# A two-layer vision block on one core: the end of a sample as a third line of steps beside the next sample's convolutions

## What is computed

```
h   = exp(d_t[..., None] * A) * h + (d_t * u_t)[..., None] * b_t[:, :, None, :]
y_t = einsum('bhkdn,bkn->bkd', h, c_t)        # over 4096 positions
yv  = ys[0] + flip(ys[2]) + wh2hw(ys[1]) + wh2hw(flip(ys[3]))
yv  = _ln(yv, out_norm_g, out_norm_b) * silu(z)
out = interleave(xl_out, yv @ out_proj_w.T) + x
```

## Time and profile before

| what | value |
|---|---|
| median of 3 runs (lowest to highest) | 19739.79 us (19717.09 to 19748.55) |
| profiled execution, its own time | 19722.72 us |
| its span, first to last instruction | 19720.9 us |
| busy share of the span: PE, DVE, ACT, POOL | 75%, 80%, 42%, 51% |
| DMA share of the 16 DMA engines | 61% |
| mean granted PE clock | 0.816 of 2.4 GHz |

### The profile page before, as it was taken

How to read it: one execution, slowest core, us unless ns; L and a number is a source line. 1 busy time by engine, 2 the same in 40 slices (tenths; PEclk the granted TensorE clock), 3 DMA queues, 4 the chain that set the end, 5 groups by cost and what they waited for, 6 DMA issues and landing times. The chain is left out here.

```text
span 19720.9 us, 211923 instructions
## 1 busy us (share of the span) xinstructions
PE 14827.0 (75%) x65784; PEld 6380.2 (32%) x65784; DVE 15739.8 (80%) x12143; ACT 8193.2 (42%) x14246; POOL 10055.0 (51%) x5172
## 2 busy tenths in 40 slices
PE   7877788587885879767796778958789487885655
PEld 4423432234322443234332333314333144321102
DVE  3338989789797897878877798878978779797995
ACT  3244335443354433634335443444334443354332
POOL 2125755457354563546644465444645447354663
PEclk9988898688986889868897788978889688886555
DMA  2226666666557665576655766556655666567775
GB/s 81 85 84 173 185 174 164 177 174 184 151 161 186 168 190 144 159 181 174 182 147 155 183 178 175 154 159 179 180 163 150 174 177 182 151 161 178 188 184 132
DMA packets 1510551, 3218.40 MB, mean 163 GB/s; under 512 B 238225, under 2 KB 669393, under 8 KB 1507921
## 3 DMA queue, kind: packets, MB, share of 16 engines
q1 hardware_dynamic: 1509456, 3204.84, 60.9%
HBM read 2473.07 MB, written 731.12 MB: 162 GB/s over the span
## 5 line engine op out<-in xcount | busy, mean ns | idle before, releaser
L1852 POOL TENSOR_TENSOR HC<-H,BR 128x1024 f32<-128x1024 f32 x3072 | 7317.8, 2384 | 5965.8 <-DVE H L1705 3282.9
L1705 DVE TENSOR_TENSOR_SCAN H<-dA,CR,PU 128x1024 f32<-128x1024 f32 x2304 | 5400.5, 2344 | 261.4 <-ACT CR L1080 58.8
L750 PE MATMUL PU<-PT,SELB 96*128 96x512 bf16 x6144 | 2264.8, 457 | 3143.6 <-DVE H L1705 2588.6
L1080 ACT ACTIVATE dA<-dA,A 128x1024 f32<-128x1024 f32 x3072 | 3506.1, 1143 | 2173.1 <-DMA dA<-dld 2149.3
L1449 DVE TENSOR_TENSOR PU<-PU,BR 128x1024 f32<-128x1024 f32 x3072 | 3731.9, 1215 | 420.4 <-PE PU L750 382.0
L750 PE MATMUL PB<-RA,RB 128*128 128x64 f32 (+4 forms) x11424 | 3881.5, 487 | 74.7 <-DVE RA L1452 43.5
L750 PE MATMUL PY<-HC,CB 128*32 128x256 f32 x24576 | 2397.1, 469 | 21.6 <-POOL HC L1852 18.8
L750 PEld LDWEIGHTS PB<-RA,RB 128*128 128x128 f32 (+3 forms) x11424 | 1753.8, 184 | 1899.6 <-issue 1766.7
L750 PEld LDWEIGHTS PU<-PT,SELB 96*128 96x128 bf16 x6144 | 501.3, 103 | 4720.3 <-issue 4128.5
L1705 DVE TENSOR_TENSOR_SCAN H<-dA,PU 128x1024 f32<-128x1024 f32 x768 | 1755.0, 2285 | 341.8 <-ACT CR L1080 228.5
L750 PE MATMUL PB<-RA 128*128 128x384 f32 (+2 forms) x4272 | 1760.9, 551 | 10.0 <-DVE T L1449 9.7
(11 more groups left out here) (165 smaller groups left out, 17187.5 us busy)
## 6 DMA issues: line engine op xcount, KB each, us to landing
dA<-dld SPq DMA_DIRECT2D x3072, 512.0 KB, 5.9
PT<-ptd SPq DMA_DIRECT2D x2304, 64.0 KB, 4.3
BR<-bcd SPq DMA_DIRECT2D x256, 512.0 KB, 7.3
ptd<-RA SPq DMA_DIRECT2D x176, 576.0 KB, 3.9
y0d<-RA SPq DMA_DIRECT2D x512, 192.0 KB, 8.0
RA<-y0d SPq DMA_DIRECT2D x128, 768.0 KB, 6.4
yd<-YS SPq DMA_DIRECT2D x768, 128.0 KB, 4.7
tkd<-RB SPq DMA_DIRECT2D x256, 262.0 KB, 4.8
```

Of the source, the lines that this page charges most:

```text
L750: return nc.tensor.matmul(out, w, x, start=start, stop=stop, skip_group_check=True)
L1080: return ac.activation(out, in_, f, **kw)
L1705: v.tensor_tensor_scan(h, a, x, 0.0 if first else K.CR[:, gi:gi + 1], MUL, ADD).then_inc(S["s_scan"], 1)
L1852: po.tensor_tensor(K.HC[:, w % NHC, :], K.H[:, w % NH, :], K.BR[:, (w // 24) % NBR, 1, :], MUL).then_inc(S["s_mulC"], 1)
```

## The change

**The lines.** The round has two lines now, `start` (a to f) and `end` (g and h). For the middle rounds a new set of tables, `AMID`, lays the steps of `end` between those of `start`, per engine. The result is laid between the scan's slots by new `TAKEN` tables. In the middle rounds the end stands where part d does. The end's own order changes too: the five stages `g.total`, `g.mean`, `g.var`, `h.gates` and `h.final` follow each other by strip, each one strip behind the one before.

**How many scans of a middle round stand in each part on DVE's list** (start, g and h are parts of their own before; after, g and h are in d's stretch):

| part | start | g | h | a | b | c | d | e | f |
|---|---|---|---|---|---|---|---|---|---|
| before | 8 | 20 | 18 | 55 | 141 | 32 | 56 | 53 | 5 |
| after | - | in d | in d | 51 | 140 | 57 | 68 | 49 | 19 |
| round 1, before | - | - | - | 67 | 141 | 62 | 63 | 45 | 8 |

**The end by strips.** The reciprocal root is taken strip by strip (two activations on 512 columns instead of two on 4096 for the whole). `XM` has three buffers of one strip; `SQ`, `RS`, `ZB`, `XB` and `LB` have one each. In a middle round the end's PSUM steps all use one bank (the third), and d's steps take turns on the other two. `g.begin` loads direction 3 whole (six DMAs of 512 KB), and direction 1 in eight pieces of three DMAs of 128 KB, five pieces at once and three after POOL has added the first three. POOL's eight adds are in groups of five and three.

**Smaller edits.** `d.in` loads straight into the padded image `YP` (rows of 64 elements, 256 bytes) and ACT works in place; before, it loaded strips of 512 elements into `XT`. The convolution weights of part d move from `RB` to `PX` and are padded from 96 to 128 output columns. `x1d` and `xld` get three buffers. `e.begin` waits for the end; `a.begin` no longer does.

```diff
     def last(self):
         yield from self.step("g.begin")
-        yield from self.woven(8, "g.load", "g.total", "g.mean", None, "g.var")
-        yield from self.step("g.rstd")
-        yield from self.woven(8, "h.load", "h.gates", "h.final")
+        stages = ("g.total", "g.mean", "g.var", "h.gates", "h.final")
+        for r in range(8 + len(stages)):
+            for q in range(len(stages) - 1, -1, -1):
+                if 0 <= r - q - 1 < 8:
+                    yield from self.step(stages[q], r - q - 1)
+            for name, i in (("g.load", r), ("h.load", r - 3), ("h.rest", r - 4)):
+                if 0 <= i < 8:
+                    yield from self.step(name, i)
...
+def merged(start, end, kind, engine):
+    left = iter(start)
+    steps = []
+    for step, n in zip(end, AMID.get((kind, engine), [0] * len(end))):
+        steps += itertools.islice(left, n)
+        steps.append(step)
+    out, left = [], iter(steps + list(left))
     slots = [("s", u, p) for u in range(NU + LAG + 1) for p in range(3)]
...
+                if pre and fin and step[0][0] in "gh":
+                    bank = NP - 1
+                else:
+                    turn = (turn + 1) % (NP - 1 if pre and fin and step[0][0] == "d" else NP)
+                    bank = turn
...
     def g_var(i, p):
         ac.wait_ge(*R.at("var", i + 1, "g"))
-        act(K.VR[:, strip(i)], R.bank(("g.var", i, 0))[0:96, :], ACT.Copy).then_inc(S["vr"], 1)
+        if i:
+            ac.wait_ge(S["h_n"], 2 * i)
+        else:
             ac.preload_act_table_set("natural_log_exp_and_others")
+        act(K.RS, R.bank(("g.var", i, 0))[0:96, :], ACT.Ln, bias=K.ONE[0:96, 1:2]).then_inc(S["vr"], 1)
+        ac.wait_ge(*R.at("vr", i + 1, "g"))
+        act(K.RS, K.RS, ACT.Exp, scale=-0.5).then_inc(S["rstd"], 1)
...
-            mm(o[:, 1::2], K.XT[:, i % 2, 0, s_], K.WP[:, 0:96], False, False)
+            mm(o[:, 1::2], K.XM[i % 3][:, s_], K.WP[:, 0:96], False, False)
...
-        dma(K.XT[:, i % 2, 0, :], K.x1d[par, 0, :, strip(i)], f"xt{i % 2}")
+        dma(K.YP[:, 0, 1 + 8 * i:9 + 8 * i, 1:65], rows8(K.x1d[b % 3, 0, :, strip(i)]), f"xin{i % 2}")
...
     def g_begin(_, p):
         if p:
             if p == 1:
-                po.wait_ge(S["gy"], 192)
+                po.wait_ge(S["gy"], 336)
+            if p == 6:
+                po.wait_ge(S["gy3"], 144)
             s = slice((p - 1) * 1024, p * 1024)
-            po.tensor_tensor(K.RB[0:96, s], K.RB[0:96, s], K.RA[0:96, s], ADD).then_inc(S["g_y13"], 1)
+            po.tensor_tensor(K.RB[0:96, s], K.RB[0:96, s], K.TY[(p - 1) % 5], ADD).then_inc(S["g_y13"], 1)
...
     def e_begin(_, p):
         if p == 0:
             take_over(po, R, "d")
+            take_over(po, R, "h")
```

More of the change, by code:

```diff
@@ L58, in parts @@
 def parts(name, i):
-    if name in ("a.load", "a.side", "b.fetch", "b.store", "c.load", "e.load", "e.norm", "g.load", "h.load"):
+    if name in ("a.load", "a.side", "b.fetch", "b.store", "c.load", "e.load", "e.norm", "g.load", "h.load", "h.rest"):
         return [0.0]
@@ L180 @@
[L180 to L184, removed]
@@ L469, in __init__ @@
         self.K, self.scan, self.fin, self.pre = K, scan, fin, pre
-        self.phases = (("g", "h") if fin else ()) + (tuple("abcdef") if pre else ()) + (("s",) if scan else ())
-        self.steps = order_of(fin is not None, pre is not None)
+        self.phases = (tuple("abcd") if pre else ()) + (tuple("gh") if fin else ()) + (tuple("ef") if pre else ()) + \
+            (("s",) if scan else ())
+        self.start = start_of() if pre else []
+        self.end = end_of() if fin else []
         self.kind = "last" if pre is None else "first" if fin is None else "middle"
-        self.use, uses = {}, []
-        for step in self.steps:
+        self.banks, last, turn = {}, {}, 0
+        d = next((n for n, step in enumerate(self.start) if step[0] == "d.begin"), 0)
+        for step in self.start[:d] + self.end + self.start[d:]:
             for j, (name, n) in enumerate(emptied(*step)):
-                self.use[step, j] = len(uses)
-                uses.append(self.at(name, n, step[0][0]))
-        self.uses = uses
+                if pre and fin and step[0][0] in "gh":
[3 more added lines that the diff above has]
+                    bank = turn
+                self.banks[step, j] = bank, last.get(bank)
+                last[bank] = self.at(name, n, step[0][0])
     def order(self, engine):
-        return merged(self.steps, self.kind, engine) if self.scan is not None else self.steps
+        if self.scan is None:
+            return self.start + self.end
+        return merged(self.start, self.end, self.kind, engine)
     def at(self, name, n, phase):
@@ L493, in bank @@
     def bank(self, step, j=0):
-        return self.K.PB[self.use[step, j] % NP]
+        return self.K.PB[self.banks[step, j][0]]
     def before(self, step, j=0):
-        n = self.use[step, j]
-        return self.uses[n - NP] if n >= NP else None
+        return self.banks[step, j][1]
     def landed(self, name):
@@ L728, in take_over @@
         e.wait_ge(*R.at(name, of, phase))
-def before_first(R):
-    return "h" if R.fin is not None else "start"
 def tensor_round(K, R):
@@ L1382, in scalar_round @@
           "e.inproj": e_inproj, "e.side": e_side, "e.conv": e_conv, "f.begin": f_begin, "f.project": f_project,
-          "f.steps": f_steps, "f.soft": f_soft, "f.split": f_split, "s": s_slot, "g.mean": g_mean, "g.var": g_var,
-          "g.rstd": g_rstd, "h.gates": h_gates, "h.final": h_final}
+          "f.steps": f_steps, "f.soft": f_soft, "f.split": f_split, "s": s_slot, "g.mean": g_mean,
+          "g.var": g_var, "h.gates": h_gates, "h.final": h_final}
     for name, i, p in R.order("ACT"):
@@ L2013, in e_load @@
             sp.wait_ge(*R.at("xm", i - 1, "e"))
-        dma(K.XT[:, i % 2, 0, :], K.x1d[par, 1, :, strip(i)], f"xt{i % 2}")
+        dma(K.XT[:, i % 2, 0, :], K.x1d[b % 3, 1, :, strip(i)], f"xt{i % 2}")
     def e_inproj(i, e):
```

442 lines of the change are left out of this document (235 added, 207 removed), and 7 rows, old and new, of the table SHARED.

## The result

The changed kernel takes **19266.2 us** (median of 4 runs, 19263.6 to 19287.6) against 19735.0 us for the kernel before. The ratio is 0.9765, with a 95% interval of 0.9748 to 0.9782. The forecast was 19310 (18990 to 19670). The profiled run took 19287.6 us, the slowest of the four, with a span of 19285.8, 435 us less than the span before (19720.9).

The account below looks back on a forecast made before the run. Neither DVE (80% busy) nor PE (75%) was named the limit; scans stood where DVE was full. From 19722.7 us, middle rounds took off 369, round 8 5 and round 9 40: 19309, say 19310 (range 18990 to 19670).

Parts of the forecast that it names:

- the slower first add: In d, a strip's first add of the end still takes between 2.6 and 3.3 us.
- the clock above 0.85 in d: In d's stretch with the end, PE's clock stays above 0.85.
- f near 250: Part f of a middle round, with 19 scans, takes near 250 us.
- The load wait: Start of d: DVE waits behind the end's queued loads, taken as 16 us a round, bounds 0 and 30.
- The term 274: Part e of a middle round: 288.2 us less four scans at 3.51 us each, 274 us.
- the 23 us of idle time taken over from round 1: Part f: 228 us of DVE work plus some 23 us idle as in round 1, 251 us.
- Rival 4: Part f: exp waits behind groups of four softplus on ACT, f 41 us longer, 19555 us in all; chance 0.10.
- at most h's PE work is hidden, at least nothing: Round 9: overlapping g and h strip by strip gains between nothing and 82 us; 40 us was taken.
- Rival 3: End in d: 32 uses of one PSUM bank stall PE, 124 us a round, 20053 us in all; chance 0.10.
- Rival 2: Part d: PE's clock falls to 0.69, 61 us more a round, about 19670 us in all; chance 0.12.
- Rival 5: Part d: loads with 256-byte rows take twice 5.5 us, 44 us over eight rounds, 19353 us in all; chance 0.05.
- That gap of 164 us a round is what there is to win: Middle rounds against round 1: the end costs 219 us of time for 55 us of DVE work, 164 us winnable.

Follow-up runs that it names:

- e10_e_after_mult: Changed kernel with 17 groups of e's convolution steps moved, on DVE alone, one instruction later, behind the PU<-PU,BR multiplication: 19378.0 us.

## Why the prediction was right, and where not

The time was 44 us under the forecast, well inside the range (22 us under it in the profiled run). But that closeness is in part luck, the sum of errors of both signs. In the profiled runs the middle rounds gained 153 us more than forecast (522 against 369), and the other four rounds came out 132 worse (87 lost, where 45 were to be gained). Of the signs that the prediction named, the slower first add, the clock above 0.85 in d and f near 250 did not come; the others did.

- **a, b, c.** 320, 681 and 380 were forecast, 322.8, 684.9 and 381.3 measured. The price of a scan taken from two densities of the same part was good enough. (The row "before" of the table of scans adds up to 388: a scan that runs across the edge of a window was counted in both. By where they start, h has 17, a 54, b 140 and f 4, together 384. By that, a's term is 325 us and not 320, the end's DVE work 91 and not 87, and c's term is untouched.) Without the end, too, the front keeps what its 46 scans cost: 165 us, where 161 and some 5 were expected.
- **d.** 378 forecast, 380.5 measured. The load wait is 22.0 against 16 (bounds 0 to 30). PE is busy for 319.4 us against 304, at a clock of 0.83, not over 0.85; the matmuls of the 68 scans take 102.6 of it, not 85. DVE's work is 326.5, where 326 and 7 for slower adds were expected. The first add is faster than it was and not slower: 1477 ns, not 2.6 to 3.3 us.

```profile
L1482 DVE TENSOR_TENSOR XT<-XT,B 96x1024 f32<-96x1024 f32 x8 | 11.8, 1477 | 5.4 <-POOL RB L1897 5.4
L1482 DVE TENSOR_TENSOR RA<-RA 96x512 f32<-96x512 f32 x16 | 21.0, 1326 | 0.3 <-ACT RA L1119 0.3
```

But in d the gate (second row) and the scaling (1249 ns) take about twice the 0.67 us that such an instruction takes when POOL does not multiply. All the end's DVE work is 67.5 us in round 9, some 94 at the front and 90 in d: the slowing went from the adds to the gates and fell by some 4 us in all, where 7 more were forecast. The prediction also names the subtractions as slowed by the Trainium skill's rule of two SBUF inputs (GPSIMD Engine Reference, Specifications). They read one of their inputs from PSUM, so that rule leaves them out, and the row agrees: 677 ns in d, 680 in the earlier trace rows.

- **e.** The term 274 was built on the old price of e's other steps. DVE has 238.4 us of work there, against 274.4 before; four scans fewer are 14 us of the 36. The other 22 are not scans: they are waits for POOL's multiplication that went, as e10_e_after_mult shows by bringing 24.5 back. Idle time took half of it again (24.6 us against 13.8).
- **f.** DVE's work was forecast at 228 and is 224.0. The step that failed is the 23 us of idle time taken over from round 1: with 19 scans among the split steps DVE is idle for 3.5 us. Both misses, e's and f's, made the round shorter. Rival 4 did not happen: ACT is busy for 168 us of 227, and DVE, not ACT, sets f.
- **Rounds 0, 1 and 8.** "0", "0" and "-5" were forecast, +13, +12 and +13 measured. Round 0 without a scan varies from 1486 to 1506 us between the kernels here that don't touch it, so its 13 mean nothing. Round 8 reads 1527 to 1531 us in the three kernels with the old end and 1532 to 1543 in all with the new: some 8 us dearer. Round 1 reads 2153 to 2161 and 2159 to 2171: some 9 dearer. The reasons were not looked for.
- **Round 9.** The term that failed outright: "at most h's PE work is hidden, at least nothing". The lower bound was wrong, since the strip-by-strip order through single buffers was slower here than the two passes. The words in which the bound was given named the mechanism (single buffers and in-order waits), but no loss was allowed for it. It cost 49 us, and with SP's order turned round it is a gain of 16.
- **The rivals.** Rival 3 had a price of 3.9 us for each of 32 uses; DVE waited 1.8 us in all. Rival 2 was nearer: the clock fell to 0.83, not to 0.69. Rival 5: beside no end (round 1), the 256-byte rows land in 7.0 us, the old ones in 6.3; that is 0.7 us, not 5.5 (in round 0, 3.1 against 2.6). By the Trainium skill's 512 bytes (DMA: Bandwidth & Descriptors, Specifications) they would be slower, and the rows agree in sign. In d of round 5 they land in 10.2 us against 5.5, but the `dA` fetches there take 8.2 against 4.8, so that says little of the length of a row. The lines of round 1, after and before:

```profile
RA<-x1d SPq DMA_DIRECT2D x8, 192.0 KB, 7.0
```

```profile
XT<-x1d SPq DMA_DIRECT2D x10, 192.0 KB, 6.3
```

- **The mechanism as a whole.** "That gap of 164 us a round is what there is to win" took round 1 for a middle round without an end. It is none: the kernel before without its end takes 2242.5 us a round, not 2157, so the end costs 138 us there and not 219, and the rest is how the scans lie. The forecast put the whole gain on the scans' places. The kernels without the end split the 87 us that were won into 45 that are mostly those places and 41 for an end that is cheaper in d, where its waits fall into idle time that d has anyway.

## What to carry to other kernels

Cost a move twice: once for the work that moves, and once for the work that can now stand elsewhere; two kernels with the moved work left out measure the split directly. When stages are woven strip by strip through single buffers, follow one turn of the ring through every in-order queue, the DMA queue above all, before giving it a lower bound of zero: here the order of 17 loads a strip was worth 70 us. And an order written out for five in-order engines is one object: the four kernels in which scans and steps of the middle rounds were displaced against each other on all engines lost 400 to 780 us, and 17 groups moved by one instruction on DVE alone cost 112 us in one kernel and nothing in the other.

## What the runs showed of the hardware

A DVE instruction with two operands in SBUF that starts while POOL multiplies does not run more slowly; it stands until POOL's instruction has ended. In part g of the kernel before:

```profile
10959.49 2.36 POOL L1852 TENSOR_TENSOR HC<-H,BR 128x1024 f32<-128x1024 f32 x1 [2.34 <-PE PY L750]
```

```profile
10960.45 2.48 DVE L1449 TENSOR_TENSOR XT<-XT,B 96x1024 f32<-96x1024 f32 x1
```

POOL ends at 10961.85 and the add at 10962.93, 1.08 us later, a little less than the add takes alone (1.22 us in the earlier trace rows). It is the same whenever the add starts: of the 56 adds of this kind that start under POOL's multiplication in the kernel before, 53 end 1.08 or 1.09 us behind it, and most of them take between 2.3 and 3.4 us. All 103 instructions `T<-RA,WH,T` (512 columns) that start so end 0.55 us behind it. It holds in the other direction too. In the changed kernel the add starts first, keeps its 1.20 us, and POOL's multiplication takes 3.24 us instead of 2.35; then the next adds (1.98 us for two elsewhere) take 4.04:

```profile
12061.93 1.20 DVE L1482 TENSOR_TENSOR XT<-XT,B 96x1024 f32<-96x1024 f32 x1
12063.17 4.04 DVE L1482 TENSOR_TENSOR XT<-XT,RB 96x512 f32<-96x512 f32 x2
```

```profile
12062.10 3.24 POOL L1887 TENSOR_TENSOR HC<-H,BR 128x1024 f32<-128x1024 f32 x1 [1.21 <-DVE H L1738]
```

Instructions with an operand in PSUM (`PU<-PU,BR`, `T<-T,PB`, and the scan) keep their 1.2, 0.68 and 2.3 us beside POOL. The forecast priced this as a slowing that grows with POOL's busy share; what decides is whether POOL is multiplying at the moment the instruction starts. The Trainium skill (SBUF — State Buffer, SBUF: two separate sides) says that GpSimd and VectorE share a pair of ports to SBUF, that this pair is "an **exclusive lock**, not a bandwidth split", and that whoever starts first holds it for the whole instruction; these rows agree. If each kind of DVE instruction is taken at the tenth percentile of its lengths over the run, what lies above it comes to 159 us of round 5 before and 161 after, and 141 and 155 of that are in instructions that start while POOL works. So most of this cost, 7 to 8% of DVE's work, is still there.
